# Three pieces of VectorE's work in the first turn of the experts, each moved behind a later gated product

## The reference, cut to what matters

```python
nx = x * rsqrt(mean(x * x) + EPS) * norm_w
probs = softmax(t @ gate_w.T); topw, topi = top_k(probs, 2)
weights = sum(one_hot(topi, E) * (topw / sum(topw))[..., None], axis=1)
h1 = base1[None] + 2 * einsum('etr,efr->etf', einsum('td,erd->etr', t, a1), b1)   # h3 likewise
act = silu(h1) * h3
out_e = einsum('etf,df->etd', act, w2) + 2 * (low rank part with a2, b2)
out = einsum('te,etd->td', weights, out_e)
```

## Time and profile before

| What | Value |
|---|---|
| Median of 3 runs | 948.76 us (948.66, 948.76, 949.9) |
| The profiled execution: its own time | 947.22 us |
| Its span | 945.5 us |
| Mean granted TensorE clock | 0.982 of full speed |
| PE busy | 869.1 us, 92% |
| DVE busy | 731.6 us, 77% |
| ACT busy | 538.2 us, 57% |
| POOL busy | 464.6 us, 49% |
| First and last gated product (L2419, 64 in all) start at | 673.2 and 929.5 us |

### The profile page before, as it was taken

How to read it: one execution, slowest core, us unless ns; L and a number is a source line. 1 busy time by engine, 2 the same in 40 slices (tenths; PEclk the granted TensorE clock), 3 DMA queues, 4 the chain that set the end, 5 groups by cost and what they waited for, 6 DMA issues and landing times. The chain is left out here.

```text
span 945.5 us, 18329 instructions
## 1 busy us (share of the span) xinstructions
PE 869.1 (92%) x6457; PEld 576.7 (61%) x6457; DVE 731.6 (77%) x1482; ACT 538.2 (57%) x791; POOL 464.6 (49%) x620
## 2 busy tenths in 40 slices
PE   5899999998887787699999999998899999999997
PEld 4777777784666555344454454453557767766775
DVE  6888899878899995988988988987665646555542
ACT  4677778888565655377777777767523123222311
POOL 4123323224587776345666656455364355345444
PEclk9999999999999998789999999999999999999999
DMA  9200000000000007655536445200000000000000
GB/s 290 71 12 12 11 11 11 11 1 0 5 1 12 9 4 139 139 119 116 115 78 135 93 100 108 51 4 15 12 1 24 9 14 22 22 0 22 11 12 11
DMA packets 35639, 43.35 MB, mean 46 GB/s; under 512 B 4825, under 2 KB 27769, under 8 KB 35569
## 3 DMA queue, kind: packets, MB, share of 16 engines
q1 hardware_dynamic: 35569, 42.43, 19.0%
HBM read 21.21 MB, written 15.07 MB: 38 GB/s over the span
## 5 line engine op out<-in xcount | busy, mean ns | idle before, releaser
L1861 ACT ACTIVATE PT<-PS 128x1024 f32<-128x1024 f32 x160 | 162.8, 1023 | 56.1 <-PE PS L1646 55.8
L1924 POOL TENSOR_SCALAR_AFFINE_SELECT PT<-PT 128x256 f32<-128x256 f32 (+1 forms) x224 | 96.9, 448 | 108.4 <-ACT PT L1861 106.2
L2351 POOL TENSOR_TENSOR PRE_sb<-PRE_sb,VA 128x512 f32<-128x512 f32 x64 | 82.2, 1284 | 132.5 <-DVE PRE_sb L2419 132.4
L2317 ACT ACTIVATE sg_d<-PS 128x512 f32<-128x512 f32 x64 | 38.2, 597 | 160.0 <-PE PS L1385 160.0
L2419 DVE TENSOR_TENSOR PRE_sb<-sg_d,PS 128x512 f32<-128x512 f32 x64 | 44.0, 688 | 85.4 <-ACT sg_d L2317 84.7
L459 ACT ACTIVATE E<-PS,m 128x512 f32<-128x512 f32 x128 | 85.7, 688 | 36.4 <-PE PS L345 27.6
L1964 DVE TENSOR_REDUCE negm<-PS 128x2 f32<-128x1024 f32 x64 | 77.8, 1221 | 21.3 <-PE PS L1635 20.4
L1661 PE MATMUL PS<-PT,VA 128*32 128x512 f32 (+3 forms) x1024 | 89.2, 444 | 0.7 <-POOL PT L1924 0.7
L1631 PE MATMUL PS<-kS,qS 48*128 48x384 bf16 (+3 forms) x512 | 73.7, 312 | 9.4 <-ACT PT L1861 2.9
L504 POOL TENSOR_SCALAR Qs<-Qs 128x1024 f32<-128x1024 f32 x32 | 34.8, 1088 | 81.6 <-ACT Qs L440 81.0
L1967 DVE TENSOR_REDUCE negm<-PS 128x2 f32<-128x768 f32 x64 | 61.2, 957 | 10.9 <-PE PS L1635 9.5
(11 more groups left out here) (331 smaller groups left out, 2310.2 us busy)
## 6 DMA issues: line engine op xcount, KB each, us to landing
qk_rows<-parts SPq DMA_DIRECT2D x32, 192.0 KB, 2.7
qS<-qk_rows SPq DMA_DIRECT2D x32, 192.0 KB, 4.4
kS<-qk_rows SPq DMA_DIRECT2D x32, 192.0 KB, 4.8
xs_sb<-XN_sb SPq DMA_DIRECT2D x20, 256.0 KB, 2.3
qk_rows<-parts SPq DMA_DIRECT2D x32, 128.0 KB, 2.8
X_sb<-in_x_dram SPq DMA_DIRECT2D x8, 256.0 KB, 6.6
qk_rows<-parts SPq DMA_DIRECT2D x32, 64.0 KB, 2.5
out_dram<-X_sb SPq DMA_DIRECT2D x8, 256.0 KB, 2.3
```

The lines of the kernel that those rows point to most:

```text
L1861: nc.scalar.activation(PT[:, quad % 2, u, :], PS[:, b:b + 2, :].rearrange("p b n -> p (b n)"), ACT.Exp).then_inc(exp_ready, 1)
L1924: nc.gpsimd.affine_select(out=v, in_=v, pattern=[[0, 4 if u == 4 else 2], [1, P]], compare_op=ALU.is_ge, fill=0.0, base=0, channel_multipl ...
L2351: nc.gpsimd.tensor_tensor(acts[:, s, f, :], acts[:, s, f, :], W[:, slot, s, :], ALU.mult).then_inc(weighted, 1)
```

## The change: what it does

In turn 0 alone, three pieces of VectorE's queue change place. `select` for sequence 1 goes from behind product 1 to behind product 2. `apply(LAST - 1)` goes from behind product 2 to behind product 3. `add_att`, with its statistics, goes from behind product 2 to behind product 4. No instruction is added or removed, and no wait. In all later turns the order stays what it was.

```diff
                     if first and n == 0:
                         divide()
                     elif first and n == 2:
+                        ex.select(dve, i + 1)
+                    elif first and n == 3:
                         apply(LAST - 1)
+                    elif first and n == 4:
                         add_att()
                     if n == 0 and not last:
                         ex.keep_x_low(dve, i + 1, 1 - slot)
@@
                         if not last:
                             ex.rank_experts(dve, i + 1)
                             keep_u_low(i + 1)
-                            ex.select(dve, i + 1)
                         if not first:
+                            if not last:
+                                ex.select(dve, i + 1)
                             add_out(i - 1)
```

## The result

| | before | changed |
|---|---|---|
| Median, 14 runs each | 948.87 us | 951.26 us |
| Profiled execution, its own time | 947.22 us | 950.08 us |
| Its span | 945.5 us | 948.3 us |

The changed kernel is slower by 2.39 us: the ratio is 1.0024, with a 95% interval of 1.0015 to 1.0033. One execution of all that are reported here, a run of the kernel `hold` further down, took 4653.61 us and is left out of that kernel's median and ratio.

The account below looks back on a forecast made before the run. TensorE was taken to bound later turns without a gap, with slack only in turn 0. A later start of `hidden(5)` (+1.0) and the clock (+1.3) gave +2.3 us on 948.76, so 951.1 us, range 949.0 to 952.4.

Parts of the forecast that it names:

- The place: Turn 0: the start of `hidden(5)` decides, with `att_added` its last condition; 692.60 against 691.58, +1.0 us.
- `select` beside GpSimd: Behind product 2, `select` waits for GpSimd's instructions: a new cost of 2.03 to 2.43 us, entered as 2.23.
- two cases: `select` lasts 3.47 us if L1465 waits for GpSimd's second instruction, 3.87 us if L1462 does, not 1.44.
- The norm: Behind product 3, beside GpSimd again: 3.82 us from the product's start to the next instruction; bound 1.71 without meeting.
- The sum: VectorE's chain from product 2 at 683.11 to `hidden(5)` at 692.60, against 691.58 before: +1.0 us.
- The clock: TensorE's idle time of some 4.8 us ahead of `hidden(5)` drops its clock to half there: +1.3 us, bounds 0 to 3.0.
- A: Rival: waits as forecast, but no clock fall on the path, or before's runs pay as often; +1.0, 949.8 us; chance 0.20.
- B: Rival: GpSimd does not hold `select` up; `hidden(5)` at 691.0, -0.6, with the slow clock 949.4 us; chance 0.12.
- C: Rival: VectorE's tiny instructions win the port and GpSimd waits; `hidden(5)` at 689.0, -2.6, 946.2 us; chance 0.05.
- D: Rival: a further GpSimd instruction is met (+1.3), or all of `hidden(5)` runs slow; 952.3 to 952.7 us; chance 0.08.

Follow-up runs that it names:

- hold: Changed kernel, but GpSimd begins weighting product 2 only when the norm of sequence 6 is done; 945.89 us, ratio 0.9967 to before.
- sum_first: Kernel before, with the sum split from its statistics and put right behind product 2, norm and statistics behind product 4; 947.47 us, ratio 0.9980 to before.
- sum_third: Changed kernel, with the sum split from its statistics and put behind product 3, norm and statistics behind product 4; 947.39 us, ratio 0.9977 to before.
- norm_sum_alone: Kernel before, with only the norm moved behind product 3 and the sum behind product 4, `select` left in place; 950.55 us, ratio 1.0022 to before.
- fill: Changed kernel plus 16 TensorE matmuls on constants in turn 0 behind the turned selection, result overwritten; 949.22 us, ratio 0.9996 to before.
- select_alone: Only `select` goes behind product 2; norm, sum and statistics follow it there as in the kernel before; 950.72 us, ratio 1.0019 to before.

## Why the prediction was right

**The place.** It named the start of `hidden(5)` as the one number that decides, and `att_added` as its new last condition. The trace agrees (4.76 us, ended by L2406), and hold, sum_first and sum_third, which bring that start forward, bring the time down with it (the last two give part of it back later).

**`select` beside GpSimd.** I had two cases, 3.47 and 3.87 us. It took 3.52: L1461 still got in, L1462 and L1465 waited, as the first case has it. I entered the middle, 0.15 too much. That the cast L1464 might wait I had named, but I read from L1458 that casts don't. That reading was weak: the row of GpSimd merges two instructions, and the first alone ran from 643.71 to 644.12, so the cast, at 644.05, met only its last 0.07 us and had started ahead of the second. sum_third shows a cast waiting, and product 3 there comes 4.25 us behind product 2, near the 4.29 (687.4 - 683.11) that I gave for that case. That GpSimd is the cause is shown by hold (1.44 us in the same order).

**The norm.** I kept the pattern of before, 3.82 us from the product's start to the next instruction; 3.77 was measured. hold shows the same cause (1.11). In rows 6, the source of my 1.11, GpSimd was idle, not at work on tiny operands as the heading says: its last instruction had ended at 707.10.

**The sum.** The chain from product 2's start (683.39) to TensorE's start (692.61) took 9.22 us; I had 692.60 - 683.11 = 9.49. So the start came +0.76 later and not +1.0.

**The clock.** The fall moved onto the path as forecast. It cost 1.83 us in the profiled execution; a like stretch in before gave 1.58, and I entered 1.3. This term is the one that was sized too small, and the start the one sized too large; they offset each other within 0.3 us, and that the total came so near is in part luck. My reason for 1.3, that some executions of before pay for a fall as well, was not tested by an experiment: a profile shows one execution of each kernel. What the traces do show is that the place of a fall differs between executions: from 330 to 335 us, ahead of every edit, the granted clock was 0.66 in before and 1.00 in sum_first, and behind the stall of 2.23 us ahead of `hidden(4)` it fell in before and in norm_sum_alone, but not in sum_first. The difference of the two profiled times (2.86) is larger than that of the medians (2.39), which would fit it and proves nothing.

**The rivals.** A (no fall on the path) is refuted by the windows and by fill. B and C (GpSimd holds nothing up, or loses) are refuted by L1462 and L1465. D's further meeting did not come.

What I had not seen is that either half of the change alone costs much of the whole (1.5 and 1.3 us of 2.4). By medians, with intervals of about 1 us to either side, whether the two add up can't be told. In the profiled executions they don't: the down projection is 2.11 and 2.01 us later in the halves, and 2.59 with both. Either half alone already puts a fall onto `hidden(5)` (2.10 and 1.59 us longer than in before, against 1.83 with both), and that can be paid only once.

## What to carry to other kernels

When a piece of VectorE's work is moved behind an instruction that sets GpSimd going, ask what of it has two SBUF inputs or is a `tensor_scalar` or a cast from SBUF: each such instruction, however tiny, can cost a whole instruction of GpSimd. Ask of a queue not only how much stands ahead of what the bounding engine waits for, but whether its idle time will lie in one piece right ahead of work that bounds: in select_alone `hidden(5)` started where it did before, but behind one stall of 4.00 us in place of 2.23 and 1.35, and 2.1 us were lost. And look for the one instruction that is waited for: splitting the sum from its statistics and letting GpSimd wait was worth 4.5 us, where reordering whole pieces lost 2.4.

## What the runs showed of the hardware that I had not expected

- VectorE's instructions of four and eight elements per partition took 1.27 (1.26 in fill) and 1.14 us in place of 0.17 beside a GpSimd instruction of 512, and ended within 0.04 us behind it, in three kernels alike (changed, fill, select_alone). In sum_third L1461 and the cast L1464 were the ones that waited, 1.28 us each.
- The Trainium skill ("SBUF — State Buffer", section "Who interferes with whom") lists casts among the instructions that can take the shared pair if their operands meet certain conditions. sum_third agrees: the cast L1464 (float32 to bfloat16, eight elements), started 0.06 us behind GpSimd's sum, took 1.28 us. In the changed kernel, started 0.02 us ahead of it, it took its usual 0.19.
- The clock fell behind a stall of 1.79 us where one of 2.23 us had gone before (norm_sum_alone), and stayed at full behind one of 2.23 us alone (sum_first), behind 1.76 us (hold), and in fill, where 16 matmuls on constants took up 3.90 us of the time ahead of `hidden(5)`.
